# Gated cross-attention block on one core: value products of a group in one run, maxima copied by ACT, a running FFN maximum, far queries split by GpSimd

## What is computed

```
x = x + tanh(g_xattn[0]) * time_warping_alignment(ctx, layernorm(x))
x = x + tanh(g_ffn[0])   * L0_ffn(layernorm(x))
x = x + tanh(g_xattn[1]) * L1_attention(layernorm(x), ctx, ctx)
x = x + tanh(g_ffn[1])   * L1_ffn(layernorm(x))

L0_ffn:  h = bit_linear(x, w1); h = silu(depthwise_conv3(h) + b); bit_linear(h, w2)
         bit_linear scales each token by 127 / max|token|, rounds, multiplies by ternary weights
L1_attention: 16 heads of 16, q = (x Wq + bq) / 4, softmax(q k^T) v, then Wo and bo
L1_ffn:  three gelu layers, each followed by a top-k selection
```

## Time and profile before

| | us |
|---|---|
| median of 3 runs | 580.42 (579.89 to 580.88) |
| the profiled execution's own time | 581.3 |
| its span | 579.6 |
| busy in the span: PE, DVE, ACT, POOL | 403.9, 414.0, 261.1, 81.3 |

### The profile page before, as it was taken

One profiled execution on the slowest core, in us unless ns is written; L12 is line 12 of the kernel. 1 busy time (PEld: TensorE's weight loads), 2 busy tenths in 40 slices (PEclk: granted clock), 3 DMA queues, 4 the chain that ended last, 5 costly groups with the idle time before them and its releaser, 6 DMA issues.

```text
span 579.6 us, 10039 instructions
## 1 busy us (share of the span) xinstructions
PE 403.9 (70%) x3352; PEld 268.5 (46%) x3356; DVE 414.0 (71%) x1680; ACT 261.1 (45%) x674; POOL 81.3 (14%) x209
## 2 busy tenths in 40 slices
PE   2898799722249799787899999999999602503106
PEld 2557586511137455454577776676545300202003
DVE  7644999999965758997988887784354575375773
ACT  3854444712231543246465555765453352353440
POOL 6791000000024063724000000000000000000000
PEclk9998799955559799799999999999999955855556
DMA  9700003287004688410034847920860000000002
GB/s 271 230 1 1 0 2 120 94 174 158 14 2 132 105 153 159 128 50 1 2 54 69 217 68 139 185 79 2 332 247 1 1 0 2 0 1 1 1 1 63
DMA packets 33448, 47.22 MB, mean 81 GB/s; under 512 B 5477, under 2 KB 29942, under 8 KB 32246
## 3 DMA queue, kind: packets, MB, share of 16 engines
q1 hardware_dynamic: 33398, 46.58, 32.9%
HBM read 37.87 MB, written 8.60 MB: 80 GB/s over the span
## 4 chain that ended last, share of the span: by engine, by line
PE 45%; DVE 33%; ACT 12%; issue 5%; POOL 4%; DVEq 0%; POOLq 0%; ACTq 0%
PE ps L2118 8%; ACT below L1726 6%; PE ps L2082 5%; DVE PR L1028 4%; PE ps L2069 4%; PE ps L2058 4%; PE ps L1967 4%; PE ps L2044 3%; DVE R L962 2%; PE ps L1912 2%; DVE prod L1024 2%; PE ps L1828 2%; DVE PR L1026 2%; PE ps L2239 1%; DVE R L958 1%
## 5 line engine op out<-in xcount | busy, mean ns | idle before, releaser
L1242 DVE TENSOR_REDUCE negm<-ps 112x1 f32<-112x375 f32 x128 | 65.5, 543 | 9.2 <-PE ps L2058 6.0
L1700 ACT ACTIVATE E<-ps 125x448 f32<-125x448 f32 x96 | 52.0, 544 | 40.9 <-PE ps L2069 40.6
L2207 PE MATMUL ps<-cnt,same 128*128 128x7 bf16 (+3 forms) x36 | 6.2, 171 | 70.9 <-ACT below L1726 62.8
L2058 PE MATMUL ps<-ks,qs 96*112 96x375 bf16 x128 | 42.8, 345 | 1.7 <-DVE negm L1242 0.8
L1230 DVE TENSOR_REDUCE acts<-gel 128x4 f32<-128x448 f32 x32 | 19.8, 621 | 31.2 <-ACT gel L1668 31.2
L2082 PE MATMUL ps<-E,v 125*32 125x112 f32 x768 | 42.0, 270 | 0.0
L2069 PE MATMUL ps<-qs,ks 99*125 99x112 bf16 x384 | 39.4, 225 | 1.2 <-DVE qs L1263 0.7
L2069 PEld LDWEIGHTS ps<-qs,ks 99*125 99x125 bf16 x384 | 33.7, 137 | 10.2 <-issue 6.2
L2207 PEld LDWEIGHTS ps<-cnt,same 128*128 128x128 bf16 (+1 forms) x36 | 4.0, 111 | 73.6 <-issue 73.6
L1668 ACT ACTIVATE gel<-ps 128x448 f32<-128x448 f32 x32 | 17.3, 544 | 29.3 <-PE ps L2118 29.3
L768 POOL CAST kp<-kx 128x750 bf16<-128x750 f32 x8 | 6.5, 812 | 163.5 <-ACT path L1583 125.1
(11 more groups left out here) (369 smaller groups left out, 1037.7 us busy)
## 6 DMA issues: line engine op xcount, KB each, us to landing
ks<-key_parts SPq DMA_DIRECT2D x48, 187.5 KB, 6.7
piwT<-fn_process_input_weights SPq DMA_DIRECT2D x4, 2048.0 KB, 14.9
key_parts<-kp SPq DMA_DIRECT2D x48, 93.8 KB
ctx_again<-in_ctx SPq DMA_DIRECT2D x7, 512.0 KB
keys<-kx SPq DMA_DIRECT2D x16, 187.5 KB, 2.2
kx<-keys SPq DMA_DIRECT2D x8, 375.0 KB, 6.0
ctxP<-in_ctx SPq DMA_DIRECT2D x8, 256.0 KB, 6.4
patT<-in_L_ffn_input_patterns SPq DMA_DIRECT2D x1, 2048.0 KB, 13.2
```

Source lines behind the costliest of these rows:

```text
L1242: drain(dve.tensor_reduce(negm[:, n:n + 1], bank(nm)[0:S, 0:SC], AX.X, ALU.max, negate=True), nm)
L1700: drain(fn(E[:, (KCH * f + c) % 6, :], bank(nm)[0:KC, 0:4 * S], ACT.Exp), nm)
L2058: fill(mm(bank(nm)[0:S, 0:SC], qs[0:SR, u // 4 % 3, n, :], ks[0:SR, u // 4 % 3, n, :], start=True, stop=True), nm)
```

## The change

Four edits:

1. *Running maximum.* ACT writes the absolute value of tiles 0 to 5 back over `ct0`, and DVE takes a running maximum of these in iterations 4 to 8 of its loop. `hmax2` and the two long reductions are gone. TensorE transposes the maximum directly behind tile 6, and the keep-clock products between them become 4 instead of 10, ahead of tile 7.
2. *Queries.* Only the first half is prepared before the loop; the second half's transposes and products move into steps -4, -3 and -2, and GpSimd splits the far queries, ahead of adding the bias. The keep-clock products of steps -5 to -2 are gone.
3. *Maxima rows.* ACT copies them instead of DVE.
4. *Value products.* The three chunks stand together behind the maxima group; the query stack moves ahead of the third score product.

```diff
+            for t in range(2):                                  # GpSimd, after the last split_keys
+                wait_drained(pool, ("qT", t, 1))
+                far = slice(448, 896)
+                did(pool.tensor_tensor(qx32[:, t, far], qx32[:, t, far], qp[:, t, 0, far], ALU.subtract))
+                settle()
+                did(pool.tensor_copy(qp[:, t, 1, far], qx32[:, t, far]))
+                settle()
+                pool.tensor_tensor(qp[:, t, 2, far], qx32[:, t, far], qp[:, t, 1, far], ALU.subtract
+                                   ).then_inc(q_far_split, 1)
...
-                if c in (5, 8):
-                    e = c - 5
-                    dve.wait_ge(silu_done, e + 3)
-                    three = hs[:, e:e + 3, :].rearrange("p c t -> p t c")
...
+                if 4 <= c < HT + 1:
+                    e = c - 3
+                    dve.wait_ge(size_ready, e + 1)
+                    if e == 1:
+                        ins = tt(hmax[:, :], ct0[:, 0, :], ct0[:, 1, :], ALU.max)
+                    else:
+                        settle()
+                        ins = tt(hmax[:, :], ct0[:, e % 3, :], hmax[:, :], ALU.max)
...
+                if c < HT - 2:                                  # ACT, behind Silu and spread_taps
+                    act.wait_ge(silu_done, c + 1)
+                    fn(ct0[:, c % 3, :], hs[:, c, :], ACT.Abs).then_inc(size_ready, 1)
...
+                if f == -4:                                     # ACT, in the attention loop
+                    norm_columns(1)
+                if f in (-3, -2):
+                    query_columns(1, f + 3)
...
+                    if c == 2 and 0 <= f + 1 < 4 * B:           # ACT, behind the query stack's copy
+                        nm = ("negT", f + 1)
+                        wait_filled(act, nm)
+                        n = 4 * ((f + 1) % 4)
+                        drain(fn(qs[SR:SR + 3, (f + 1) // 4 % 3, n:n + 4, :].rearrange("p n s -> p (n s)"),
+                                 bank(nm)[SR:SR + 3, 0:4 * S], ACT.Copy), nm)
...
-            keep_clock(("hidT", HT - 1, 0), 10)
-            pe.wait_ge(hmax_part, 2)
+            pe.wait_ge(hmax_ready, 1)
             hidden_transposes(("hmaxT",), hmax)
+            keep_clock(("hidT", HT - 1, 0), 4)
...
-                if f < 0:
+                if f == -4:
+                    ln_transposes(2, "lnT2", ln2, 1)
+                if f in (-3, -2):
+                    query_product(1, f + 3)
+                if f == -1:
                     keep_clock(("pv", 0), 3)
...
-                if behind:
-                    value_products(f - 1, 0)
                 if now:
                     scores_less_maximum(f, 1)
+                if f + LAG + 1 < 4 * B:
+                    queries(f + LAG + 1)
                 if ahead:
                     scores_for_maximum(f + LAG, 2)
-                if f + LAG + 1 < 4 * B:
-                    queries(f + LAG + 1)
                 if 0 <= f + 1 < 4 * B:
                     maxima(f + 1)
                 if behind:
-                    value_products(f - 1, 1)
+                    for c in range(KCH):
+                        value_products(f - 1, c)
                 if ahead:
                     scores_for_maximum(f + LAG, 3)
                 if now:
                     scores_less_maximum(f, 2)
-                if behind:
-                    value_products(f - 1, 2)
```

More of the change, by code:

```diff
@@ L360, in build_program @@
         hmax = rf.take("hmax", [128, TOK])
-        hmax2 = rf.take("hmax2", [128, TOK])
         q2 = Region(q2_at).take("q2", [128, HT, TOK], BF16)
@@ L1121, in _ @@
                               ALU.mult, ALU.add), nm)
[L1122 to L1128 removed]
+                if 4 <= c < HT + 1:
[3 more added lines that the diff above has]
+                        ins = tt(hmax[:, :], ct0[:, 0, :], ct0[:, 1, :], ALU.max)
                     else:
[L1130 removed]
                         settle()
[L1132 to L1134 removed]
+                        ins = tt(hmax[:, :], ct0[:, e % 3, :], hmax[:, :], ALU.max)
+                    if e < HT - 3:
+                        did(ins)
+                    else:
+                        ins.then_inc(hmax_ready, 1)
             def token_maxima(j, nm):
@@ L1211, in _ @@
                 normalise(b, x, ln2[:, b, :])
-            for half in range(2):
-                for t in range(2):
-                    wait_drained(dve, ("qT", t, half))
-                    cols = slice(448 * half, 448 * half + 448)
-                    did(tt(qx32[:, t, cols], qx32[:, t, cols], qp[:, t, 0, cols], ALU.subtract))
-                    settle()
-                    did(dve.tensor_copy(qp[:, t, 1, cols], qx32[:, t, cols]))
-                    settle()
-                    tt(qp[:, t, 2, cols], qx32[:, t, cols], qp[:, t, 1, cols], ALU.subtract).then_inc(q_split, 1)
+            near = slice(0, 448)
+            for t in range(2):
+                wait_drained(dve, ("qT", t, 0))
+                did(tt(qx32[:, t, near], qx32[:, t, near], qp[:, t, 0, near], ALU.subtract))
+                settle()
+                did(dve.tensor_copy(qp[:, t, 1, near], qx32[:, t, near]))
+                settle()
+                tt(qp[:, t, 2, near], qx32[:, t, near], qp[:, t, 1, near], ALU.subtract).then_inc(q_split, 1)
             a0 = quarters(acts[0][:, :])
@@ L1257, in _ @@
                             ALU.mult, ALU.add).then_inc(x_ready, 1)
-                    if i == 2 and 0 <= f + 1 < 4 * B:
-                        nm = ("negT", f + 1)
-                        wait_filled(dve, nm)
-                        n = 4 * ((f + 1) % 4)
-                        drain(dve.tensor_copy(qs[SR:SR + 3, (f + 1) // 4 % 3, n:n + 4, :].rearrange("p n s -> p (n s)"),
-                                              bank(nm)[SR:SR + 3, 0:4 * S]), nm)
                 if t == 0 and 1 <= b <= B - 1:
@@ L1642, in norm_columns, with query_columns @@
                     drain(fn(ln2T[:, h, 448 * half:448 * half + 448], bank(nm)[:, 0:448], ACT.Copy), nm)
-            def query_columns(half):
-                for t in range(2):
-                    nm = ("qT", t, half)
-                    wait_filled(act, nm)
-                    cols = slice(448 * half, 448 * half + 448)
-                    did(fn(qx32[:, t, cols], bank(nm)[:, 0:448], ACT.Identity, bias=bqs[:, t:t + 1], scale=HD ** -0.5))
-                    drain(fn(qp[:, t, 0, cols], bank(nm)[:, 0:448], ACT.Identity, bias=bqs[:, t:t + 1],
-                             scale=HD ** -0.5), nm)
+            def query_columns(half, t):
+                nm = ("qT", t, half)
+                wait_filled(act, nm)
+                cols = slice(448 * half, 448 * half + 448)
+                did(fn(qx32[:, t, cols], bank(nm)[:, 0:448], ACT.Identity, bias=bqs[:, t:t + 1], scale=HD ** -0.5))
+                drain(fn(qp[:, t, 0, cols], bank(nm)[:, 0:448], ACT.Identity, bias=bqs[:, t:t + 1],
+                         scale=HD ** -0.5), nm)
             half_root(2, 0)
@@ L1658, in _ @@
             normalise(2, ln2, 1, 2)
[L1659 to L1661 removed]
+            query_columns(0, 0)
+            query_columns(0, 1)
             def gelu(i):
@@ L2023, in _, with query_product @@
                 keep_clock(("lnT2", 0, 0), 3)
-            for half in range(2):
-                ln_transposes(2, "lnT2", ln2, half)
+            def query_product(half, t):
+                nm = ("qT", t, half)
+                claim(pe, nm)
                 for h in range(DH):
                     wait_drained(pe, ("lnT2", h, half))
-                for t in range(2):
-                    nm = ("qT", t, half)
-                    claim(pe, nm)
-                    for h in range(DH):
-                        ins = mm(bank(nm)[:, 0:448], wqT[:, h, 128 * t:128 * t + 128],
-                                 ln2T[:, h, 448 * half:448 * half + 448], start=(h == 0), stop=(h == DH - 1))
-                    fill(ins, nm)
+                    ins = mm(bank(nm)[:, 0:448], wqT[:, h, 128 * t:128 * t + 128],
+                             ln2T[:, h, 448 * half:448 * half + 448], start=(h == 0), stop=(h == DH - 1))
+                fill(ins, nm)
+            ln_transposes(2, "lnT2", ln2, 0)
+            query_product(0, 0)
+            query_product(0, 1)
             def queries(u):
@@ L2040, in queries @@
                 tile = u % 4 // 2
-                pe.wait_ge(q_split, 2 * (u // (2 * B)) + tile + 1)
+                pe.wait_ge(q_split if u < 2 * B else q_far_split, tile + 1)
                 for i in range(4):
```

16 lines of the change are left out of this document (4 added, 12 removed).

## The result

| | before | after |
|---|---|---|
| median us (range, 6 runs each) | 581.04 (579.89 to 583.65) | 577.00 (574.11 to 579.24) |
| profiled execution: time, span | 581.3, 579.6 | 579.24, 577.5 |

The changed kernel takes 0.9925 of the time before, 95% interval 0.9904 to 0.9946, or 4.4 us less (0.0075 x 581). I had predicted 8.0 less; 577.0 lies inside the range. The profiled execution of the changed kernel was the slowest of its six.

A forecast was written before the change was run, and what follows sets the result against it. The prediction took TensorE to bound the attention loop, DVE the first FFN's end and attention's start; -2.0 - 3.4 - 2.6 = -8.0 us on 581.3, with the profiled execution 0.9 above the median, gave 572.4, range 566.5 to 578.

The forecast's parts named there:

- Running maximum: End of the first FFN: token reductions end 2.6 us earlier, GpSimd takes some back at the scaling steps, -2.0 us.
- Rival B: GpSimd blocks DVE's new maxima, scaling steps and maxima split; FFN gain -0.3, attention start -2.0, 575.5 us; chance 0.18.
- Start of attention: First query split to first scoreT product: the first score reduction comes 5.4 us earlier, net -3.4 us, bounds -1.5 and -5.4.
- +1.9: Start of attention: DVE idles about 0.9 and 1.0 us in steps -3 and -2, waiting for query products ahead of the scores.
- -0.6 and +0.7: Start of attention: two unlabelled terms; the text beside gives 0.7 back for the maxima copy, up to 0.9 for their split.
- rival C: TensorE's clock falls to 1.2 GHz from 267 us and stays through the first steps; no gain or about 583; chance 0.04.
- first scoreT near 283: Start of attention: listed sign of being right, the first scoreT product near 283 us, against 286.34 before.
- A step of attention: Attention loop: -0.35 us per step on TensorE, less new waits; steps about 3.27, 4.3, 3.3 and 4.3 us.
- Each wait that I had named: Attention loop: TensorE waits 0.15 us for the exponential at t=0, for pvs at t=1, 0.4 for the x sum at t=3.
- the loop's sum: Attention loop: all step terms, +0.8 at step 21 and +0.2 for the last steps give -2.6 us, bounds 0 and -9.5.
- Rival A: Attention loop: full return without new waits, -9.5 us instead of -2.6, 565.5 us in all; chance 0.10.
- Rival D: Attention loop: ACT's maxima copy is late every step, 0.3 us x 27 eats the gain, 580.4 us; chance 0.06.

The follow-up runs named there:

- e2: The kernel before with the query edit alone (far half moved into the loop's first steps, split by GpSimd): 580.63 us, ratio 0.9991.
- e7: The changed kernel with GpSimd's far splits held behind the first maxima split and more keep-clock products at the start of attention: 578.79 us, ratio 0.9949 to before.
- e11: The changed kernel with the mended start (later far splits, more keep-clock) and ACT's pvs copy ahead of the third exponential: 574.39 us, ratio 0.9898 to before.
- e12: The changed kernel with mended start, earlier pvs copy, and key and pattern loads spread out: 573.50 us, ratio 0.9864 to before.
- e3: The kernel before with the loop's edits alone (maxima rows copied by ACT, value products in one run): 581.24 us, ratio 0.9998.
- e5: The changed kernel without the key loads of sequences 3 to 7, values not the reference's: 572.69 us, ratio 0.9848 to before.
- e6: The kernel before without the key loads of sequences 3 to 7, values not the reference's: 581.10 us, ratio 1.0004.
- e4: The changed kernel with ACT's pvs copy moved ahead of the step's third exponential: 574.75 us, ratio 0.9889 to before.
- e9: The changed kernel with each key stack loaded in two lots a step apart and the patterns in four pieces: 576.42 us, ratio 0.9906 to before.
- e1: The kernel before with the running FFN maximum alone: 584.52 us, ratio 1.0044.

## Why the prediction was right, and where it was not

The direction and the range held; the size was off by 4.6 us of 577. Step by step:

- **Running maximum: right.** -1.93 in the profile against -2.0. The end of the token reductions and the collision of both scaling steps with GpSimd came as written; so did the maxima, but for the one that met a GpSimd subtraction (2.30), which TensorE didn't notice. Rival B in its full form is out.
- **Start of attention: the mechanism right, one term missing.** The sum's +1.9 for the far half inside the steps left the clock out. (Its -0.6 and +0.7 seem to be the copy's gain and the split's cost, for which the text beside it has 0.7 and up to 0.9. The copy gave 0.85: 1.21 us from its product to scoreT against 2.06 in e2.) I had judged "the new order is denser" and kept the fall of the clock for rival C. It fell, for 3.4 us: rival C in small. With the clock kept (e7, e11, e12) the stretch is 16.26 each time, -3.4 as forecast. My line "first scoreT near 283" didn't follow from my own sum, which gives 286.34 - 5.4 = 280.9; it came at 283.73.
- **A step of attention: the terms under-sized.** The t = 0 step takes 3.21 (3.27 forecast), t = 2 3.21 (3.3), t = 1 4.15 (4.3), t = 3 4.27 to 4.37 (4.3): -0.86 in four steps without stalls, where the forecast's terms add up to -0.5. Each wait that I had named is there: the exponential, pvs, x. The wait behind step 21 is too: steps 22 and 23 are 4.97 and 4.90, +0.6 over before. Only the last steps cost more, 2.30 + 3.90 + 2.62 against 8.31 (+0.5; I had +0.2).
- **What failed is the loop's sum,** which took TensorE to be held by its own order and by other engines' latencies alone, and put the key loads at nothing. e3 and the changed kernel have 3.7 and 5.8 us of issue waits, before 0.7. In the changed kernel 2.3 of them are waits for a key stack, which had landed only 0.36 to 1.93 us ahead of its use before, and the new steps bring that use forward by some 1.2 us (11.6 to 10.4); 3.5 have no semaphore and each ends 1.4 us behind an instruction transfer. In the profile they took back all of the loop's gain but 0.26; e5 against e6 gives the whole change's gain without the loads, 8.4 us. That this is near the forecast of 8.0 is in part luck: between those two profiles the three stretches gain 3.4, 1.6 and 5.7 us, half clocks included, against 2.0, 3.4 and 2.6 forecast.
- **Rival A** is out, by the waits that e5 still shows. **Rival D** is out: no wait in ordinary steps is for the maxima copy (L1706 has 0.2 us, once).
- **Not forecast:** +0.8 ahead of the change's first instruction. The clock came back later in the stretch from 174 to 178, with a mean of 0.64 after and 0.80 before, which is the likely cause:

```profile
174.00:178.00 4.00, 4.00 (x14) 2.99 (x13) 0.96 (x3) 0.00 (x0) 3.84 (x4) 0.64 0.09 25
```

Nothing was changed there, and other executions of the changed order (e4, e5) reach the first tap at 200.4 to 200.7. So one profile carries an uncertainty of some 2 us in this stretch alone (200.2 in e9 to 202.8), and a change of 4 us can't be read off one pair of spans. The +0.8 in the rest stays unexplained.

## What to carry to other kernels

An engine that is 99% busy hides more than other engines' latencies: shorten its work and ask what feeds it, loads of data first and perhaps its own instructions, since loads that cost nothing before may then cost much of the gain; leave the loads out once to see it. Where a view puts a wait down to nobody, look in the kernel for the semaphore that stands ahead of the instruction, and compare the landing of the DMA behind it with the instruction's start: here that named 2.3 of 5.8 us in the changed kernel, and 4.8 of 5.7 in the fastest one. And before shortening a loop, read how long each load has been there when it is used. Where work moves to the head of a stage, look for short bursts with pauses on TensorE, and price the clock as a term of the sum and not as a far rival. Measure parts in their own stretch as well as by the median, since here every part worked where it stood in one profile at least and none alone moved the median down clear of the noise.

## What was not expected of the hardware

- Thirty loads of 187.5 KB in the loop cost 0 us (e6) with TensorE 99% busy, and 4.3 us (e5) with its work made shorter. A stack of six takes 10.1 to 11.7 us from its first issue to its last landing, and the product that waits for it starts 0.08 to 0.10 us behind the landing. Without the loads no such wait is left, and none of the next kind either.
- The waits that no semaphore explains, 0.6 to 3.65 us each, end 1.26 to 1.67 us behind the end of a 16 KB instruction transfer, 15 times out of 15.
- The stretches at 1.2 GHz come at other places in each kernel's profiled execution: before 240.5 to 247.3, after 269.1 to 272.5, e1 283.0 to 286.5, e6 287.0 to 293.8. The last two come behind a stretch in which TensorE paused: in e6 it is busy for 1.00 of the 2 us from 284 to 286, in e1 for 1.90 of the 3 from 280 to 283. They probably make up much of the spread of some 5 us between executions of one kernel: in the 68 of the kernel before that were timed beside e1 to e12, the slower ones have the lower mean granted clock (0.832 to 0.846, correlation -0.6).
- A DVE operation of 112 x 4 or 112 x 16 elements takes 0.17 to 0.19 us alone, and 0.89 to 1.46 beside a GpSimd operation on large tiles, with which it ends (235.84 and 238.01; 281.48 against 279.97 in e7).
